# A four-sequence transformer block with a top-k mask on one NeuronCore: where five small pieces of work stand

## The chip, the cores and the metric

One NeuronCore of a Trainium2 chip runs the whole program. The metric is the device time of one execution in microseconds (us). Engines are named as the profile names them: PE is TensorE (PEld its weight loads), DVE is VectorE, ACT is ScalarE, POOL is GpSimd, SP is SyncE, which issues most DMAs. The five engines run their own instruction lists and meet only at semaphores.

## The reference

Four sequences of 512 rows of 512 numbers. For each sequence, first a mask from a top-k, then a transformer block:

```python
adj = emb_s * emb_t * softmax(x, axis=-1) / sqrt(512)      # 512 x 512 per sequence
adj[diag] = -inf
x = x + (1.0 where adj is among its 5120 largest of the sequence, else 0)
ada = timestep_embed @ ada_w + ada_b                        # shift, scale, gate, twice
x1 = ln(x) * (1 + scale1) + shift1
q, k, v = x1 @ qkv_w + qkv_b                                # 16 heads of 128
attn_out = softmax(q k^T / sqrt(128)) v                     # then @ out_w + out_b
y = x + gate1 * attn_out
x2 = ln(y) * (1 + scale2) + shift2
y = y + gate2 * (gelu(x2 @ ffn_w1 + b1) @ ffn_w2 + b2)      # hidden width 2048
out = x + y
```

All is float32. The kernel gets that precision from TensorE by splitting each operand into a high and a low part and adding three products.

## The kernel before

**The matrix work.** The program is written out for sequences 0, 1, 2, 3, one after the other. Every product is three matmuls (`mm3`: high by high, high by low, low by high; L1387, L1388, L1389), each 128 by 128 weights against 512 columns (256 where only half of the rows is done, `ROWS[0]` or `ROWS[1]`). In a head h PE does: 12 matmuls of scores q k^T, then q and k of head h+1 (24), one tile of v for head h+4 (12), and the product of probabilities and v of head h-1 (12, `attend`, done is counted in `pv_done`): 60 in all. From head 12 on v tiles give way to pieces of the output projection. After head 15 come the rest of that projection (`wide(b, "out", u, ...)`, u = 0 to 3, 16 pieces `kc` each, result columns in four banks of PSUM), its way back (`transpose_back`), the second layer norm (z), `mlp_in` and `mlp_out`.

**The weights.** Halves of 1 MB are loaded by SP into four places, (region 0 or 1, half 0 or 1), from a DRAM scratch in which they lie split. Only sequence 0 finds them unsplit: there ScalarE writes the high part (`split_hi`), then GpSimd the low part (`split_lo`, L661), and saves follow. A unit of the output projection is two such halves: half 0 holds kc 0 to 7, half 1 kc 8 to 15.

**The softmax of a head** runs on three engines: VectorE finds row maxima (L1217), ScalarE the exponentials (L884), VectorE reciprocals, ScalarE and VectorE the high and low halves of 16 bits (L891, L1232), SP transposes them with a DMA, and GpSimd widens them to `probT` (`widen`, L741). VectorE then makes the low parts of q and k of the next head (`qk_part`, L1188), without which PE can't start its scores, and the low parts of v and of the head's result.

**The top-k** of sequence b+1 runs beneath sequence b. In heads 0 to 4 VectorE finds the softmax's maxima, multiplies (`topk_adj`, L1062), and turns values into keys that sort as integers (`topk_keys`, two passes per tile, L1071 and L1073); GpSimd puts minus infinity on the diagonal between the two (`clear_diagonal`, L652). Then 32 steps of a bisection over the threshold `cand`, 16 over the keys' upper 16 bits and 16 over the lower (variable `low`): VectorE counts one half of the keys above `cand` (`cnt_v`, L1028), ScalarE the other (sum of signs, `cnt_s`, L779), PE sums both over partitions (`take_total`, L1399 and L1400), and VectorE moves `cand` (`topk_move`, L1091 and L1094). I call the sum of step s "total s". Totals 0 to 10 stand in heads 5 to 15, totals 11 to 15 amid the output projection, the others in the MLP. After total 15 VectorE makes `low` from the chosen upper level (L1105, L1108). The top-k of sequence 0 runs alone at the start and has a form of its own (`is_t0`).

What sets the order is the code of each engine, written out by hand; there is no scheduler. `wait_apart` is a wait on a semaphore in an instruction of its own.

## Time and profile before

| | us |
|---|---|
| time, median of 3 runs | 1572.07 (1571.55 to 1572.12) |
| the profiled execution's own time | 1573.86 |
| its span, first to last instruction | 1572.0 |
| PE busy in the span | 1508.5 (96%) |
| DVE busy | 1110.1 (71%) |
| ACT busy | 886.3 (56%) |
| POOL busy | 409.9 (26%) |
| PE in the chain that ended last | 87% of the span |

The busy time of PE counts overlapping matmuls once, and the end of a matmul is modelled: in a dense stretch matmuls start every 0.23 us while each is shown 0.39 us long. So lost time of PE is read from the distances of starts and from the waits, not from the busy share. Sequence 0's block begins at about 100 us, sequence 1's at 482 us, sequence 2's at 848 us, and sequence 3's at 1210 us.

### The profile page before, as it was taken

How to read it: one execution, taken by the hardware profiler on the slowest of the kernel's cores; microseconds unless marked ns; L12 is line 12 of the kernel's file. 1: busy time of each engine (PE TensorE's matmuls, PEld its weight loads, DVE VectorE, ACT ScalarE, POOL GpSimd, SP SyncE). 2: the span in 40 equal slices, each digit the busy share in tenths (PEclk: the TensorE clock that was granted, in tenths of full speed). 3: DMA queues.
4: the chain of work that ended last, by engine and by line, in shares of the span. 5: the costliest groups of instructions: out<-in, count | busy, mean ns of one | idle time of the engine just before them, and what ended most of it. 6: DMA issues, size and time to landing. Idle time of an engine off the chain costs nothing.

```text
span 1572.0 us, 21300 instructions
## 1 busy us (share of the span) xinstructions
PE 1508.5 (96%) x7253; PEld 1250.4 (80%) x7253; DVE 1110.1 (71%) x2328; ACT 886.3 (56%) x1631; POOL 409.9 (26%) x243
## 2 busy tenths in 40 slices
PE   1999889999999999999999999999999999999998
PEld 1877778778778888887878888887978888888987
DVE  7878978876786887775775887775777666664431
ACT  4557577774754666663672766664572556554240
POOL 6713635454120322221000232221000122222000
PEclk9999999999999999999999999999999999999999
DMA  7867869998666788685455777677454787776463
GB/s 289 314 242 195 237 171 261 247 219 299 216 231 238 170 214 215 165 206 176 175 219 205 199 207 208 163 214 208 168 201 170 220 201 160 209 210 156 176 237 123
DMA packets 334507, 327.58 MB, mean 208 GB/s; under 512 B 270752, under 2 KB 275008, under 8 KB 331328
## 3 DMA queue, kind: packets, MB, share of 16 engines
q1 hardware_dynamic: 334112, 325.90, 69.3%
q8 instruction: 58, 0.95, 0.2%
q14 instruction: 49, 0.40, 0.1%
q10 hardware_dynamic: 288, 0.33, 0.1%
HBM read 204.54 MB, written 54.54 MB: 165 GB/s over the span
## 4 chain that ended last, share of the span: by engine, by line
PE 87%; DVE 7%; DMA 2%; DVEq 1%; ACT 1%; issue 1%; SPq 1%; POOL 0%; ACTq 0%; POOLq 0%
PE bank L1387 26%; PE bank L1388 26%; PE bank L1389 26%; PE bank L1701 2%; DMA w<-split_weights 1%; DVE halves L1232 1%; DVE tb L1028 1%; PE bank L1604 1%; PE bank L1599 1%; PE bank L1600 1%; PE bank L1416 1%; DVEq L1218 1%; SPq L537 1%; DVE adj L1073 1%; DVE tb L1071 1%
## 5 line engine op out<-in xcount | busy, mean ns | idle before, releaser
L741 POOL CAST probT<-turned 128x2048 fp32r<-128x2048 f16 x128 | 244.3, 1924 | 700.8 <-DMA turned<-halves 395.3
L1387 PE MATMUL bank<-xT,w 128*128 128x512 f32 x704 | 281.0, 399 | 2.0 <-POOL w L661 2.0
L1388 PE MATMUL bank<-xT,w 128*128 128x512 f32 x704 | 275.6, 391 | 0.0
L1389 PE MATMUL bank<-xT,w 128*128 128x512 f32 x704 | 275.3, 391 | 0.0
L884 ACT ACTIVATE prob<-bank,nbias 128x512 f32<-128x512 f32 x256 | 176.4, 690 | 119.8 <-DVE nbias L1219 110.5
L1232 DVE SCALAR_TENSOR_TENSOR halves<-prob,rinv,halves 128x512 f16<-128x512 f32 x256 | 176.7, 752 | 25.2 <-ACT halves L891 24.9
L1217 DVE TENSOR_REDUCE rowmax<-bank 128x1 f32<-128x512 f32 x256 | 174.4, 681 | 0.0
L891 ACT ACTIVATE halves<-prob,rinv 128x512 f16<-128x512 f32 x256 | 164.1, 711 | 17.1 <-DVE rinv L1228 15.3
L1389 PEld LDWEIGHTS bank<-xT,w 128*128 128x128 f32 x704 | 133.0, 189 | 28.2
L1387 PEld LDWEIGHTS bank<-xT,w 128*128 128x128 f32 x704 | 132.9, 189 | 28.0 <-POOL w L661 2.4
L1388 PEld LDWEIGHTS bank<-xT,w 128*128 128x128 f32 x704 | 133.0, 189 | 25.5
L661 POOL TENSOR_TENSOR w<-wraw,w 128x1024 fp32r<-128x1024 f32 x38 | 95.5, 2518 | 179.2 <-ACT w L820 178.9
L1387 PE MATMUL bank<-act,w 128*128 128x512 f32 (+1 forms) x320 | 114.1, 357 | 3.8 <-DMA w<-split_weights 3.8
L1188 DVE SCALAR_TENSOR_TENSOR act<-bank,small,act 128x512 fp32r<-128x512 f32 x64 | 47.9, 748 | 94.6 <-ACT act L911 94.6
L779 ACT ACTIVATE passed_s<-adj,cand 128x1024 bf16<-128x1024 uint16 (+1 forms) x64 | 73.8, 1153 | 70.9 <-DVE cand L1094 41.1
L1388 PE MATMUL bank<-act,w 128*128 128x512 f32 (+1 forms) x320 | 111.5, 348 | 0.0
L1389 PE MATMUL bank<-act,w 128*128 128x512 f32 (+1 forms) x320 | 111.5, 348 | 0.0
L911 ACT ACTIVATE act<-bank,small 128x512 fp32r<-128x512 f32 x64 | 44.0, 688 | 116.0 <-PE bank L1389 115.9
L779 ACT ACTIVATE passed_s<-low,cand 128x1024 bf16<-128x1024 f32 (+1 forms) x64 | 74.0, 1156 | 55.4 <-DVE cand L1094 24.6
L1387 PE MATMUL bank<-qk 128*128 128x512 f32 x256 | 99.9, 390 | 5.5 <-DVE qk L1188 5.2
L1387 PE MATMUL bank<-w,act 128*128 128x512 f32 x256 | 101.5, 396 | 0.0
L1188 DVE SCALAR_TENSOR_TENSOR qk<-bank,small,qk 128x512 fp32r<-128x512 f32 x128 | 90.3, 744 | 14.9 <-ACT qk L876 8.6
(173 smaller groups left out, 3342.4 us busy)
## 6 DMA issues: line engine op xcount, KB each, us to landing
w<-split_weights SPq DMA_DIRECT2D x154, 1024.0 KB, 6.0
split_weights<-w SPq DMA_DIRECT2D x38, 1024.0 KB, 6.7
wraw<-weights_in SPq DMA_DIRECT2D x48, 512.0 KB, 4.8
split_weights<-xT SPq DMA_DIRECT2D x7, 1024.0 KB, 7.8
adaw<-ada_w_in SPq DMA_DIRECT2D x4, 1536.0 KB, 12.6
xr<-x_in SPq DMA_DIRECT2D x4, 1024.0 KB, 6.3
split_weights<-qk SPq DMA_DIRECT2D x3, 1024.0 KB, 7.8
adj<-x_in SPq DMA_DIRECT2D x3, 1024.0 KB, 7.9
```

Source lines behind the costliest of these rows:

```text
L661: nc.gpsimd.tensor_tensor(w[:, region, 1, span], wraw[:, k % 2, :], w[:, region, 0, span].bitcast(F32), ALU.subtract)\
L741: nc.gpsimd.tensor_copy(probT[:, :, :, rows].rearrange("p a j (i t) -> p i (a j) t", i=2), turned_of(h)[:, 2 * pair:2 * pair + 2, :, :]).t ...
L779: nc.scalar.activation(passed_s[:, :2 * NCOUNT - at], src, ACT.Sign, bias=cand[:, :], scale=-1.0, accum_out=cnt_s[:, :]).then_inc(counted_ ...
L884: nc.scalar.activation(prob[:, i, :], bank[i][:, :], ACT.Exp, bias=nbias[:, i:i + 1], scale=SCALE, accum_out=rowsum[:, i:i + 1]).then_inc( ...
L891: nc.scalar.mul(halves_of(h)[:, i, 0, :], prob[:, i, :], rinv[:, i:i + 1]).then_inc(p16_hi, 1)
L911: nc.scalar.activation(act[:, 0, h, :], bank[6][:, :], ACT.Identity, bias=col("bv", h))\
L1188: return V.scalar_tensor_tensor(dst, src, bias, hi.bitcast(F32), ALU.add, ALU.subtract)
L1217: V.reduce_max(rowmax[:, i:i + 1], bank[i][:, :], AX.X)
L1232: V.scalar_tensor_tensor(halves_of(h)[:, i, 1, :], prob[:, i, :], rinv[:, i:i + 1], halves_of(h)[:, i, 0, :], ALU.mult, ALU.subtract).then ...
L1387: pe.matmul(dst, w_hi_ap, x_hi_ap, start=first, stop=False)
L1388: pe.matmul(dst, w_hi_ap, x_lo_ap, start=False, stop=False)
L1389: return pe.matmul(dst, w_lo_ap, x_hi_ap, start=False, stop=last)
```

## The change

Five edits, in the order of the program:

1. **Keys ahead of q, k.** In heads 1 to 4 VectorE's top-k passes (`topk_under_head`) stand ahead of `qk_part` of the next head, instead of behind it.
2. **Clearing of the diagonal** of tiles 0 and 1 moves on GpSimd from head 0 to behind the widening of head 1, of tiles 2 and 3 from head 1 to head 2. In sequence 0 the split of unit 5's first half also waits for all eight tiles of z.
3. **One matmul for both counts.** `cnt_v` and `cnt_s` become two columns of one tile `counts`, and PE sums both with one matmul with ones (not for sequence 0's own top-k). The combination of the two sums is made by one more VectorE instruction of one column ahead of the comparison.
4. **Level change in one pass.** GpSimd scales the lower 16 bits into `low` when all heads are done (`next_low`), for each sequence as already for sequence 0's own top-k; VectorE then needs one pass over 2048 columns in place of two. The lower level's numbers are scaled by 2^-17 throughout.
5. **Unit 3's first rows amid unit 2.** PE does pieces 0 to 7 of unit 3's first rows between pieces 7 and 8 of unit 2, and the other eight where all sixteen stood.

```diff
@@ GpSimd
+            def next_low(b):
+
+                pool.wait_ge(pv_done, (b + 1) * H)
+                scale_low()
+
...
@@ GpSimd, first_sequence
                     for k in range(at + max(1, n - 1), at + n):
                         split_lo(k)
                     at += n
-                    if h < 2:
-                        clear_diagonal(1, 2 * h, 2 * h + 1)
+                    if h in (1, 2):
+                        clear_diagonal(1, 2 * h - 2, 2 * h - 1)
+                next_low(0)
                 for k in range(at, NHALF):
                     if ORDER[k] == unit_half(5, 0):
                         first_rows_lo(0)
+                        wait_apart(pool, z_ready, 2 * NT)
                     split_lo(k)
@@ GpSimd, later sequences
                     widen(b, h)
-                    if b < B - 1 and h < 2:
-                        clear_diagonal(b + 1, 2 * h, 2 * h + 1)
+                    if b < B - 1 and h in (1, 2):
+                        clear_diagonal(b + 1, 2 * h - 2, 2 * h - 1)
+                if b < B - 1:
+                    next_low(b)
                 first_rows_lo(b)
@@ VectorE, topk_move
-                    V.tensor_scalar(step_up[:, :], total(step)[:, 0:1], float(KTOP - P * NCOUNT // 2) - 0.5, bit,
-                                    ALU.is_gt, ALU.mult)
+                    bit *= unit(step)
+                    V.tensor_scalar(step_up[:, :], total(step)[:, 1:2], 0.5, float(KTOP - P * NCOUNT // 2) - 0.5,
+                                    ALU.mult, ALU.add)
+                    dve.drain()
+                    V.tensor_scalar(step_up[:, :], total(step)[:, 0:1], step_up[:, :], bit, ALU.is_gt, ALU.mult)
...
-                    if is_t0(t):
-                        dve.wait_ge(low_scaled, 1)
-                        V.scalar_tensor_tensor(low[:, :], keys16[:, :, 1], cand[:, :], low[:, :],
-                                               ALU.subtract, ALU.add)
-                    else:
-                        V.tensor_scalar(low[:, :], keys16[:, :, 1], cand[:, :], float(1 << 17),
-                                        ALU.subtract, ALU.mult)
-                        dve.drain()
-                        V.tensor_tensor(low[:, :], low[:, :], keys16[:, :, 0], ALU.add)
+                    dve.wait_ge(low_scaled, t + 1)
+                    V.scalar_tensor_tensor(low[:, :], keys16[:, :, 1], cand[:, :], low[:, :], ALU.subtract, ALU.add)
@@ VectorE, head
+                dve.drain()
+                if not last and 0 < h < FIRST_TOTAL:
+                    topk_under_head(b + 1, h)
                 if h + 1 < H:
                     qk_part(b, h + 1)
                 dve.drain()
-                if not last:
+                if not last and not 0 < h < FIRST_TOTAL:
                     topk_under_head(b + 1, h)
@@ PE, take_total
-                pe.matmul(total(step)[:, 0:1], weight_v[:, :], cnt_v[:, :], start=not is_t0(t), stop=False)
-                pe.matmul(total(step)[:, 0:1], weight_s[:, :], cnt_s[:, :], start=False, stop=True)\
-                    .then_inc(total_ready, 1)
+                if is_t0(t):
...
+                else:
+                    pe.matmul(total(step)[:, 0:2], ones[:, :], counts[:, :], start=True, stop=True)\
+                        .then_inc(total_ready, 1)
@@ PE, output projection
-                    wide(b, "out", 2, parts[r], parts[r + 1], y_done)
+                    if r == 1:
+                        wide(b, "out", 2, 6, 8, y_done)
+                        wide(b, "out", 3, 0, 8, y_done, ROWS[0])
+                        wide(b, "out", 2, 8, 10, y_done)
+                    else:
+                        wide(b, "out", 2, parts[r], parts[r + 1], y_done)
...
-                wide(b, "out", 3, 0, KC, y_done, ROWS[0])
+                wide(b, "out", 3, 8, KC, y_done, ROWS[0])
```

VectorE at the end of head 3 of sequence 0, before (L1232 the low halves, L1188 the low parts of q and k or of a head's result, L1071 and L1073 the two passes over the keys of a tile):

```order
L1232 SCALAR_TENSOR_TENSOR halves_0_69<-prob,rinv,halves_0_69 128x512 x4
L1188 SCALAR_TENSOR_TENSOR qk<-bank,small,qk 128x512 x2
L1071 TENSOR_SCALAR tb<-adj 128x512
L1073 TENSOR_TENSOR adj<-adj,tb 128x512
L1071 TENSOR_SCALAR tb<-adj 128x512
L1073 TENSOR_TENSOR adj<-adj,tb 128x512
L1183 SCALAR_TENSOR_TENSOR v<-bank,v 128x512
```

The same place after the change (lines are some five to nine further down):

```order
L1237 SCALAR_TENSOR_TENSOR halves_0_69<-prob,rinv,halves_0_69 128x512 x4
L1080 TENSOR_SCALAR tb<-adj 128x512
L1082 TENSOR_TENSOR adj<-adj,tb 128x512
L1080 TENSOR_SCALAR tb<-adj 128x512
L1082 TENSOR_TENSOR adj<-adj,tb 128x512
L1193 SCALAR_TENSOR_TENSOR qk<-bank,small,qk 128x512 x2
L1188 SCALAR_TENSOR_TENSOR v<-bank,v 128x512
```

The four passes over keys now stand between the halves and q, k.

GpSimd at the end of the heads of sequence 0, before (L661 the low part of a half unit of weights, L741 the widening of a head, L678 the low part of the first rows):

```order
L661 TENSOR_TENSOR w<-wraw,w 128x1024 x2
L741 CAST probT<-turned_1_72 128x2x8x128 x2
L661 TENSOR_TENSOR w<-wraw,w 128x1024 x5
L678 TENSOR_TENSOR xT<-tmp,xT 128x256 x4
```

And after:

```order
L661 TENSOR_TENSOR w<-wraw,w 128x1024 x2
L748 CAST probT<-turned_1_72 128x2x8x128 x2
L661 TENSOR_TENSOR w<-wraw,w 128x1024
L688 TENSOR_SCALAR low<-adj 128x2048
L661 TENSOR_TENSOR w<-wraw,w 128x1024 x4
L678 TENSOR_TENSOR xT<-tmp,xT 128x256 x4
```

The first split behind the widening is unit 2's second half; the scaling of `low` has come between it and the split of unit 3's first half.

PE in the output projection around total 13, before (L1539 turns a column block back, then the total, then pieces of unit 2):

```order
L1539 MATMUL bank<-ident,yT 128x128 x4
L1399 MATMUL bank<-cnt_v,ones 128x1
L1400 MATMUL bank<-cnt_s,minus_half 128x1
L1387 MATMUL bank<-act,w 128x512
L1388 MATMUL bank<-act,w 128x512
L1389 MATMUL bank<-act,w 128x512
L1387 MATMUL bank<-act,w 128x512
L1388 MATMUL bank<-act,w 128x512
L1389 MATMUL bank<-act,w 128x512
L1387 MATMUL bank<-act,w 128x512
```

And after:

```order
L1550 MATMUL bank<-ident,yT 128x128 x4
L1411 MATMUL bank<-counts,ones 128x2
L1395 MATMUL bank<-act,w 128x512
L1396 MATMUL bank<-act,w 128x512
L1397 MATMUL bank<-act,w 128x512
L1395 MATMUL bank<-act,w 128x512
L1396 MATMUL bank<-act,w 128x512
L1397 MATMUL bank<-act,w 128x512
L1395 MATMUL bank<-act,w 128x256
L1396 MATMUL bank<-act,w 128x256
```

One small matmul is left of two, and behind unit 2's pieces 6 and 7 the half-wide matmuls of unit 3 begin (24 of them stand there).

## Rows read from the trace of the kernel before

**Rows 1.** Busy time by stretch: time, PE, PEld, DVE, ACT, POOL, clock, DMA.
```profile
120.00:500.00 380.00, 363.73 (x1736) 297.13 (x1735) 298.72 (x571) 241.47 (x427) 152.95 (x74) 0.99 0.79 232
500.00:870.00 370.00, 367.46 (x1770) 302.93 (x1770) 271.69 (x577) 214.58 (x402) 67.36 (x40) 1.00 0.66 194
```

**Rows 2.** Waits of PE over the span: total us, times, longest.
```profile
PE bank L1399 <- DVE act L1188: 5.2, 1, 5.2
PE bank L1387 <- DMA w<-split_weights: 3.8, 3, 2.3
PE bank L1416 <- DVE z L1169: 3.1, 2, 1.9
PE bank L1539 <- DVE yT L1250: 1.5, 1, 1.5
```

**Rows 3.** PE's order of time around one total of two counts, and around take_ranks.
```profile
815.01 0.39 PE L1389 MATMUL bank<-w,act 128*128 128x512 f32 x1
...
815.69 0.39 PE L1389 MATMUL bank<-w,act 128*128 128x512 f32 x1
...
816.30 0.40 PE L1388 MATMUL bank<-w,act 128*128 128x512 f32 x1
...
821.30 0.39 PE L1389 MATMUL bank<-w,act 128*128 128x512 f32 x1
...
821.93 0.39 PE L1388 MATMUL bank<-w,act 128*128 128x512 f32 x1
```

**Rows 4.** VectorE in head 3 of sequence 0: start, length.
```profile
172.23 2.51 DVE L1071 TENSOR_SCALAR tb<-adj 128x512 int32<-128x512 int32 x1
...
181.97 0.69 DVE L1183 SCALAR_TENSOR_TENSOR v<-bank,v 128x512 fp32r<-128x512 f32 x1
```

**Rows 5.** PE starts the scores of head 5 of sequence 0.
```profile
192.25 0.47 PE L1387 MATMUL bank<-qk 128*128 128x512 f32 x1 [3.68 <-DVE qk L1188]
```

**Rows 6.** GpSimd in head 3 of sequence 0.
```profile
172.05 4.94 POOL L661 TENSOR_TENSOR w<-wraw,w 128x1024 fp32r<-128x1024 f32 x2 [5.11 <-ACT w L820]
```

**Rows 7.** Granted clock after two waits of PE: stretch, PE, PEclk, DMA.
```profile
200.50:204.00 3.50, 3.50 (x10) 0.50 0.05 19
736.40:739.90 3.50, 3.50 (x13) 0.51 0.02 7
```

**Rows 8.** VectorE in heads 1 and 3 of sequence 1.
```profile
524.01 1.41 DVE L1188 SCALAR_TENSOR_TENSOR qk<-bank,small,qk 128x512 fp32r<-128x512 f32 x2
...
527.49 0.69 DVE L1183 SCALAR_TENSOR_TENSOR v<-bank,v 128x512 fp32r<-128x512 f32 x1
...
550.30 1.40 DVE L1188 SCALAR_TENSOR_TENSOR qk<-bank,small,qk 128x512 fp32r<-128x512 f32 x2
...
554.34 0.69 DVE L1183 SCALAR_TENSOR_TENSOR v<-bank,v 128x512 fp32r<-128x512 f32 x1
```

**Rows 9.** PE starts the scores of head 4 of sequence 1.
```profile
553.55 0.39 PE L1387 MATMUL bank<-qk 128*128 128x512 f32 x1
```

**Rows 10.** GpSimd: the scaling of low, and the end of sequence 0's heads.
```profile
17.95 5.38 POOL L683 TENSOR_SCALAR low<-adj 128x2048 f32<-128x2048 uint16 x1 [4.61 <-DVE cand L1037]
...
364.87 4.75 POOL L661 TENSOR_TENSOR w<-wraw,w 128x1024 fp32r<-128x1024 f32 x2 [8.25 <-ACT w L820]
```

**Rows 11.** PE takes total 13 in sequence 0.
```profile
366.70 0.17 PE L1399 MATMUL bank<-cnt_v,ones 128*128 128x1 f16 x1
```

**Rows 12.** PE's total 15 and VectorE's level change, sequence 1.
```profile
741.33 0.18 PE L1399 MATMUL bank<-cnt_v,ones 128*128 128x1 f16 x1
...
742.10 1.29 DVE L1105 TENSOR_SCALAR low<-adj,cand 128x2048 f32<-128x2048 uint16 x1
743.46 2.29 DVE L1108 TENSOR_TENSOR low<-low,adj 128x2048 f32<-128x2048 f32 x1
...
747.83 0.81 DVE L1250 TENSOR_SCALAR yT<-bank,small,ada 128x512 f32<-128x512 f32 x1
```

**Rows 13.** PE waits for unit 2's second half in sequence 1.
```profile
735.60 0.50 PE L1387 MATMUL bank<-act,w 128*128 128x512 f32 x1 [2.33 <-DMA w<-split_weights]
```

More of the change, by code:

```diff
@@ L204, in count_split, with unit @@
     return FIRST_V if is_t0(t) else NCOUNT
-def unit(t, step):
-    return UNIT if is_t0(t) and step >= LEVEL else 1.0
+def unit(step):
+    return UNIT if step >= LEVEL else 1.0
 def first_splits(h):
@@ L312, in block_kernel @@
         offset = new("offset", [P, 1], F16)
-        cnt_v = new("cnt_v", [P, 1], F16)
-        cnt_s = new("cnt_s", [P, 1], F16)
+        counts = new("counts", [P, 2], F16)
+        cnt_v, cnt_s = counts[:, 0:1], counts[:, 1:2]
         sign_sum = new("sign_sum", [P, 1], F16)
@@ L787, in topk_sides @@
                                          accum_out=sign_sum[:, :]).then_inc(signs_summed, 1)
-                nc.scalar.mul(far_cand[:, :], cand[:, :], -FAR / unit(t, LEVEL)).then_inc(far_ready, 1)
+                nc.scalar.mul(far_cand[:, :], cand[:, :], -FAR / unit(LEVEL)).then_inc(far_ready, 1)
                 act_e.wait_ge(far_ready, t * 2 + 1)
                 act_e.wait_ge(ties_counted, t + 1)
-                nc.scalar.activation(low[:, :], low[:, :], ACT.Identity, bias=far_cand[:, :], scale=FAR / unit(t, LEVEL))\
+                nc.scalar.activation(low[:, :], low[:, :], ACT.Identity, bias=far_cand[:, :], scale=FAR / unit(LEVEL))\
                     .then_inc(far_ready, 1)
@@ L1030, in count @@
                 if is_t0(t):
-                    far = TOP_BIT / (1 << step % LEVEL) / 2 * unit(t, step)
+                    far = TOP_BIT / (1 << step % LEVEL) / 2 * unit(step)
                     V.tensor_scalar(bounds[:, 0:1], cand[:, :], -far, None, ALU.add)
@@ L1036, in start_level @@
             def start_level(t, step):
-                V.memset(cand[:, :], (TOP_BIT - 0.5) * unit(t, step)).then_inc(cand_ready, 1)
+                V.memset(cand[:, :], (TOP_BIT - 0.5) * unit(step)).then_inc(cand_ready, 1)
                 dve.drain()
@@ L1393, in take_total @@
                     pe.wait_ge(cand_ready, step + 1)
-                weight_v, weight_s = (big, minus_half_big) if is_t0(t) else (ones, minus_half)
                 if is_t0(t):
@@ L1398, in take_total @@
                 pe.wait_ge(counted_s, t * STEPS + (step + 1))
-                pe.matmul(total(step)[:, 0:1], weight_v[:, :], cnt_v[:, :], start=not is_t0(t), stop=False)
-                pe.matmul(total(step)[:, 0:1], weight_s[:, :], cnt_s[:, :], start=False, stop=True)\
-                    .then_inc(total_ready, 1)
+                if is_t0(t):
+                    pe.matmul(total(step)[:, 0:1], big[:, :], cnt_v[:, :], start=False, stop=False)
+                    pe.matmul(total(step)[:, 0:1], minus_half_big[:, :], cnt_s[:, :], start=False, stop=True)\
+                        .then_inc(total_ready, 1)
+                else:
+                    pe.matmul(total(step)[:, 0:2], ones[:, :], counts[:, :], start=True, stop=True)\
+                        .then_inc(total_ready, 1)
             def take_ranks(t):
```

## The prediction

> **What bounds the kernel now.** I read first the table of busy time by stretch [rows 1]. From 120 us on PE is the bound: in 500 to 870 it idles 2.5 of 370 us, in 120 to 500 (sequence 0) 16.3 of 380. So only two things count: work that PE itself loses or gains, and PE's waits. The list of waits, read next [rows 2], with one more row for q, k [rows 5], names them: 3.7 us and 5.2 us on VectorE in sequence 0, 1.9 on z, 1.5 on a gated column block, and three waits for weight loads, 3.8 in sum, the longest 2.3 in sequence 1 [rows 13]. Third, the clock: after the wait of 5.2 us and after that of 2.3 us stretches of 3.5 us show a granted clock of 0.50 and 0.51 [rows 7], that is 1.2 GHz of 2.4, though PE is never idle in them. Each costs half of 3.5, about 1.75 us. No such stretch follows the wait of 3.7 us at once, so a wait may or may not cost this.
>
> The pace of a full matmul is 0.227 us: three starts in 0.68 us [rows 3]. A head's 60 are 13.6 us.
>
> **One matmul for both counts.** From 815.69 to 816.30 PE starts one full matmul, the two small ones and another full one: 0.61 us, of which 0.45 are the full ones, so the pair costs 0.16. Around take_ranks, with three small ones, the same distance is 0.63 [rows 3]. One small matmul more or less is thus 0.02 to 0.03 us. There are 32 totals in each of three sequences: 96 x 0.025 = 2.4 us saved. Bounds: nothing, if the 0.16 is the price of any interruption, and 7.5 us, if half of each pair's 0.16 goes. I take 2.4, because the three-matmul row is the same situation one step further.
> The Trainium skill (TensorE: Matmul & The Clock Gate, "LDWEIGHTS (loading the stationary operand)") prices a weight load at columns/1.2 ns, 107 ns for 128 columns; were each removed load exposed, this edit would give 10 us. The rows above speak against it.
>
> **The instruction added to each step.** One more VectorE instruction of one column with its drain lies between a total and the new `cand`. From total 15 at 741.33 to the level change at 742.10 [rows 12] pass 0.77 us, in which two such instructions stand and the way over the semaphore, so I take 0.24 for one more. It is hidden where PE has 2.7 us between totals. It shows where only nine matmuls (2.0 us) stand between totals 14 and 15, and where a head's q, k were already late. I take +0.3 us beyond what is in the terms below; bounds 0 and 3.
>
> **Keys ahead of q, k, sequence 0.** In head 3 the four key passes begin at 172.23 and the next work at 181.97: 9.7 us [rows 4]. In sequence 1 the same four fill 551.7 to 554.34, 2.6 us [rows 8]. The difference is GpSimd, which splits weights from 172.05 for 4.94 us [rows 6] and then widens: the first pass took 2.51 us, which is the length of one of GpSimd's two splits. So VectorE's head 4 ran late, its q, k held PE until 192.25 [rows 5], and the count and the low part of head 3's result, behind another slow tile, until 5.2 us later [rows 2]. Put ahead of q, k the passes start 1.4 us earlier: the first tile (1.3 us) is through before GpSimd starts, the second waits out both splits to 177.0 and ends at 177.4, and q, k end at 178.8. Add 1.2 us for head 2, where the multiplications meet the split in the same way: 180.0. PE could start head 4 at 192.25 - 3.68 - 13.6 = 175.0, so a new wait of 5 us stands here. Head 5 then starts at 193.6, and the total that came after the wait of 5.2 us comes at 196.3 instead of 200.2. The slow stretch of 1.75 us stays, behind another wait. Gain 3.9, rounded to 4 us. A wait of PE on a split in head 1, which stood behind the diagonal's clearing, also goes, but head 1's q, k are as much later (two multiplications and their small instructions, 2.1 us in [rows 8]); I let these cancel. Bounds: 9 us gained if the passes meet no split, 1 lost if both tiles do.
> The Trainium skill (SBUF — State Buffer, "Who interferes with whom") says that VectorE with two SBUF inputs and GpSimd exclude each other for the whole of an instruction, and the earlier starter wins. By that rule the split delays the second tile exactly as above; the trace agrees with it (2.51 us against 2.6 for four passes).
>
> **The same in sequences 1 and 2.** No wait of VectorE's making exists there to be cured. Head 1's q, k end at 525.42 and the next work starts at 527.49, so the moved passes are 2.1 us; head 3's end at 551.7, moved passes 2.6 [rows 8]. PE starts head 4 at 553.55 [rows 9] and head 2 at 553.55 - 27.2 = 526.35. So q, k would be ready at 527.5 and 554.3: 1.1 and 0.8 us late. VectorE's work per head is unchanged (it only swaps order), so from head 2 on the lateness is mostly shared, not added: a PE that is 1.2 us late gives all of it back as slack at the next head. I get 1.3 us per sequence, 2.6 in sum. Bounds: 0, if the engine has this slack, and 8, if each of four heads adds its 1.0 us.
>
> **Level change and unit 3's rows, sequence 0.** This is the largest term and it is a loss. GpSimd is strictly in order: the split of unit 2's second half (from 364.87, half of 4.75 us, to 367.25), then now the scaling, 5.38 us as at 17.95 [rows 10], to 372.6, then the split of unit 3's first half, 2.4, to 375.0. PE takes total 13 at 366.70 [rows 11], does six matmuls, and wants unit 3 at 368.2: it waits 6.8 us, and a slow stretch adds 1.75. Behind it the split of unit 3's second half, whose high part ScalarE makes only after its count, meets VectorE's level change; PE then waits some 3.5 us for the gated block in place of 1.5 [rows 2]. The wait of 1.9 on z goes, since GpSimd now stays off. 6.8 + 1.75 + 3.5 - 1.5 - 1.9 = 8.6, of which I take 8 for what overlaps. Bounds: 2 (the wait short and unslowed) and 12.
>
> **The same in sequences 1 to 3.** Here GpSimd is free and the scaling is hidden behind unit 0 to 2's matmuls (it takes 5.4 us from the end of the last head, and total 15 comes later than unit 2's thirteenth piece). Unit 3's first half was issued ahead of the load that ends PE's wait at 735.60 [rows 13], so it is there, and 24 half-wide matmuls (2.7 us) cover the waits of 3.8 us and their slow stretch of 1.75: -5.55. But half of unit 3's cover is gone from behind total 15. VectorE's gated block ends at 748.64, 7.3 us after total 15 [rows 12]; PE had 9 matmuls and 48 half-wide ones there, about 7.7 us, and now has 24, about 4.9. The one pass costs 2.3, as a pass with two inputs does, against 1.29 + 2.29 and a gap [rows 12], so VectorE needs 7.3 - 1.35 + 0.24 = 6.2: a new wait of about 1.2 us in sequences 1 and 2, and 0.2 each at total 15. -5.55 + 2.4 + 0.4 = -2.8 us. Bounds: -5.5 and +1.
>
> **Sum.** -2.4 + 0.3 - 4 + 2.6 + 8 - 2.8 = +1.7 us. The profiled execution took 1573.86 us (span 1572.0 and 1.9 around it) and would take 1575.6; it lies 1.8 above the median of the runs, so on their scale 1572.07 + 1.7 = 1573.8 us. A difference of 0.2%, 3.1 us, is about what can be told from none.
>
> **Rivals.** (A) PE's wait for unit 3 in sequence 0 doesn't hold, because the scaling starts as soon as head 15 is done and is over by the time it is wanted. GpSimd idled 8.25 us before 364.87 [rows 10], which speaks for it; that the split of unit 2's second half stands ahead of the scaling in its list speaks against. Without the term: 1565.8 us. (B) Small matmuls cost more than the comparison of two and three shows, and half of each pair's 0.16 us goes: 5.1 us more, 1568.7. For it: the slow start of the full matmul behind a pair. Against: the same slow start behind three. (C) Slower: the lateness of q, k adds up. Place: heads 1 to 4 of sequences 1 and 2. Price: 1.0 us x 8 heads = 8 instead of 2.6, so 1579.2. It decides as soon as VectorE's moved passes (2.1 and 2.6 us) exceed the slack between q, k and the scores (0.9 us at head 2, 1.85 at head 4, [rows 8, 9]) at each head anew, which happens if its work behind q, k waits for a PE result that now comes later too. For it: the low part of a head's result does wait for PE. Against: that wait is short.
>
> **How the numbers follow.** Forecast 0.51, A 0.19, B 0.08, C 0.22. The forecast's own size is uncertain by some 4 us (the unit 3 term by 3, the head terms by 2 each), so I count 0.41 of it within 3.1 us and 0.10 slower. A and B are faster: 0.27. Slower: 0.22 + 0.10 = 0.32. Range 1565 to 1580: from A to just beyond C.
>
> **What will show it.** In the new profile: PE's full matmuls one small matmul apart 96 times; in sequence 0 one wait of about 5 us on q, k at head 4 and none before the first total of the next top-k; a wait of about 7 us on GpSimd's split near 366 to 375; no wait on weight loads; VectorE's waits of about 1 us on q, k in heads 2 to 5 of sequences 1 and 2 and on the gated block. I am wrong if the 7 us wait is missing, or if the heads of sequence 1 lose nothing.

## The result: 1581.0 us, slower by 0.55%, outside the range

| | before | after |
|---|---|---|
| median | 1572.09 us (4 runs, 1571.55 to 1572.53) | 1581.04 us (4 runs, 1577.58 to 1583.27) |
| ratio | | 1.0055, 95% interval 1.0035 to 1.0075 |
| profiled execution, its span | 1573.86, 1572.0 | 1583.27, 1581.4 |
| mean granted clock in the span | 0.996 | 0.991 (its other runs 0.993 to 0.995) |

In the terms of the sum the changed kernel is 8.6 us slower (0.0055 x 1572), where +1.7 was forecast. Measured once more in other rounds it stood at 1.0045 (1.0027 to 1.0063), +7.1 us. One execution of the kernel with edit 4 alone, 2780 us at a mean granted clock of 0.81, is left out of its median and its ratio.

The profile of the changed kernel first lists PE's waits (total us, times, longest), the answer to [rows 2]; those of the first top-k are left out:

```profile
PE bank L1395 <- DVE qk L1193: 12.5, 7, 3.7
PE bank L1395 <- POOL w L661: 7.5, 2, 6.6
PE bank L1550 <- DVE yT L1258: 4.6, 3, 1.9
...
PE bank L1427 <- DVE z L1174: 2.0, 1, 2.0
...
PE bank L1395 <- issue: 0.7, 2, 0.3
```

The wait of 5.2 us at the first total and the 3.8 us for weight loads are gone, as forecast. There are now seven waits on q, k in place of three (12.5 us for 5.2), one of 6.6 us on GpSimd's split, and three on the gated block in place of one. By stretch (time, PE, PEld, DVE, ACT, POOL, clock, DMA), the answer to [rows 1]:

```profile
120.00:500.00 380.00, 360.61 (x1668) 295.10 (x1667) 294.69 (x598) 238.55 (x424) 156.03 (x75) 0.97 0.77 223
500.00:870.00 370.00, 366.89 (x1745) 302.06 (x1744) 275.77 (x606) 213.51 (x400) 70.93 (x41) 1.00 0.67 200
```

In sequence 0 PE is busy 3.1 us less than before in the same 380 us, and while busy it has the lower clock: 0.97 against 0.99. Sequence 1's stretch is nearly as before. Sequence by sequence, by PE's first matmul of each MLP (L1599, now L1610): before they start at 389.71, 757.15, 1119.07 and 1478.51, now at 402.12, 765.88, 1130.23 and 1488.03. So sequence 0 loses 12.4 us, sequence 1 gives 3.7 back, sequence 2 loses another 2.4, and sequence 3 gives back 1.6; a second profile of the changed kernel, which loses 10.5 us in sequence 0, shows the other three within 0.2 us. Of the 12.4 us the waits account for 5.0 (19.3 for 14.3 us from 101 us on): more than half of the loss in sequence 0 is not in the list of waits at all. Here are four stretches of the changed kernel, each at or behind the end of one of its waits (same columns):

```profile
148.60:155.40 6.80, 6.62 (x17) 5.21 (x18) 4.94 (x13) 2.50 (x7) 3.29 (x4) 0.53 0.59 219
182.70:189.50 6.80, 5.86 (x15) 4.63 (x16) 5.09 (x11) 3.29 (x7) 5.27 (x3) 0.53 1.07 388
373.90:380.70 6.80, 5.97 (x27) 5.89 (x28) 0.00 (x0) 0.00 (x0) 0.77 (x1) 0.53 0.71 230
394.30:397.70 3.40, 3.40 (x20) 3.40 (x19) 2.66 (x10) 0.37 (x2) 2.61 (x2) 0.56 0.62 133
```

A full matmul starts every 0.43 us in them, every 0.23 elsewhere. With one more of 3.4 us at 101 they make 27.2 us at half clock (the second profile of the same kernel shows 20.4); before there were 13.7. The forecast had looked at two windows of 3.5 us [rows 7]; it missed a stretch behind the 2.0 us wait of head 1, and that the one in its first window begins while PE still waits:

```profile
149.40:152.80 3.40, 3.40 (x10) 2.63 (x9) 2.93 (x7) 2.92 (x7) 2.57 (x2) 0.50 0.88 308
197.20:204.00 6.80, 3.55 (x10) 2.87 (x11) 5.86 (x14) 4.89 (x11) 1.59 (x1) 0.50 0.50 201
```

These are single executions, and the profiled one of the changed kernel has the lowest clock of its four. Over all executions on record the mean granted clock is 0.9937 for the changed kernel (9 executions) and 0.9950 for the one before (92): 0.0013 of 1572 us, some 2 us.

The waits themselves, in their order. PE at head 2 of sequence 0, and what VectorE and GpSimd did there:

```profile
148.78 0.77 PE L1395 MATMUL bank<-qk 128*128 128x512 f32 x1 [3.74 <-DVE qk L1193]
```
```profile
143.60 3.57 DVE L1071 SCALAR_TENSOR_TENSOR adj<-tb,factor,adj 128x512 f32<-128x512 f32 x2
147.27 1.41 DVE L1193 SCALAR_TENSOR_TENSOR qk<-bank,small,qk 128x512 fp32r<-128x512 f32 x2
```
```profile
144.27 2.36 POOL L661 TENSOR_TENSOR w<-wraw,w 128x1024 fp32r<-128x1024 f32 x1 [7.17 <-ACT w L829]
```

Two multiplications now stand ahead of q, k and take 3.57 us, because a split starts within the first of them, 0.03 us before its end, and holds up the second; q, k end at 148.7 and PE starts at 148.78. At head 4 the wait is 3.43. The output projection of sequence 0, GpSimd and then PE, the answers to [rows 10] and [rows 11]:

```profile
364.62 2.39 POOL L661 TENSOR_TENSOR w<-wraw,w 128x1024 fp32r<-128x1024 f32 x1 [8.32 <-ACT w L829]
366.97 5.38 POOL L688 TENSOR_SCALAR low<-adj 128x2048 f32<-128x2048 uint16 x1
372.32 2.35 POOL L661 TENSOR_TENSOR w<-wraw,w 128x1024 fp32r<-128x1024 f32 x1
```
```profile
366.45 0.17 PE L1411 MATMUL bank<-counts,ones 128*128 128x2 f16 x1
...
374.73 0.58 PE L1395 MATMUL bank<-act,w 128*128 128x256 f32 x1 [6.64 <-POOL w L661]
```

This is the forecast's 6.8 us wait to 0.2 us. Behind total 15 in sequence 0 and in sequence 1, the answer to [rows 12]:

```profile
385.65 4.09 DVE L1113 SCALAR_TENSOR_TENSOR low<-adj,cand,low 128x2048 f32<-128x2048 uint16 x1
...
752.67 2.35 DVE L1113 SCALAR_TENSOR_TENSOR low<-adj,cand,low 128x2048 f32<-128x2048 uint16 x1
```
```profile
392.69 0.66 PE L1550 MATMUL bank<-ident,yT 128*128 128x128 f32 x4 [1.90 <-DVE yT L1258]
...
757.97 0.66 PE L1550 MATMUL bank<-ident,yT 128*128 128x128 f32 x4 [1.34 <-DVE yT L1258]
```

The one pass takes 2.35 us where GpSimd is free, and 4.09 where a split (385.22 to 387.60) meets it. PE waits 1.34 us in sequences 1 and 2 (forecast 1.2). The last row answers to [rows 3], a total in the MLP:

```profile
818.17 0.39 PE L1397 MATMUL bank<-w,act 128*128 128x512 f32 x1
818.40 0.18 PE L1411 MATMUL bank<-counts,ones 128*128 128x2 f16 x1
...
818.75 0.39 PE L1396 MATMUL bank<-w,act 128*128 128x512 f32 x1
```

From full to second full matmul pass 0.58 us with one small one, 0.61 with two, 0.63 with three.

### The profile page after: what moved, and what is told of

Read it like the earlier page. It is cut to its first block, busy times and chain, and to the rows that moved or that the text cites. A ratio compares the mean times of both kernels' runs of the same rounds, so it can differ in the third digit from the quotient of the medians.

```text
span 1581.4 us, 21362 instructions
## 1 busy us (share of the span) xinstructions
PE 1511.4 (96%) x7157; PEld 1253.0 (79%) x7157; DVE 1120.2 (71%) x2421; ACT 885.3 (56%) x1631; POOL 420.1 (27%) x246
## 4 chain that ended last, share of the span: by engine, by line
PE 84%; DVE 9%; DVEq 3%; ACT 1%; issue 1%; POOL 1%; DMA 1%; SPq 0%; ACTq 0%
PE bank L1395 25%; PE bank L1397 25%; PE bank L1396 25%; PE bank L1717 2%; DVE tb L1037 1%; DVE halves L1237 1%; DVEq L1223 1%; PE bank L1615 1%; PE bank L1610 1%; PE bank L1611 1%; PE bank L1427 1%; DVE low L1113 1%; DVE adj L1082 1%; PE bank L1449 1%; PE bank L1446 1%
## 5 line engine op out<-in xcount | busy, mean ns | idle before, releaser
L661 POOL TENSOR_TENSOR w<-wraw,w 128x1024 fp32r<-128x1024 f32 x38 | 94.4, 2485 | 201.4 <-ACT w L829 199.9
L1395 PE MATMUL bank<-act,w 128*128 128x512 f32 (+1 forms) x320 | 115.6, 361 | 7.5 <-POOL w L661 7.5
L1395 PE MATMUL bank<-qk 128*128 128x512 f32 x256 | 102.6, 401 | 13.2 <-DVE qk L1193 12.5
L1396 PE MATMUL bank<-act,w 128*128 128x512 f32 (+1 forms) x320 | 112.6, 352 | 0.0
L1397 PE MATMUL bank<-act,w 128*128 128x512 f32 (+1 forms) x320 | 112.6, 352 | 0.0
L1193 DVE SCALAR_TENSOR_TENSOR qk<-bank,small,qk 128x512 fp32r<-128x512 f32 x128 | 90.6, 747 | 19.3 <-ACT qk L885 7.9
L1397 PE MATMUL bank<-qk 128*128 128x512 f32 x256 | 101.6, 397 | 0.0
```

The costliest lines, as they stand in the source:

```text
L661: nc.gpsimd.tensor_tensor(w[:, region, 1, span], wraw[:, k % 2, :], w[:, region, 0, span].bitcast(F32), ALU.subtract)\
L1193: return V.scalar_tensor_tensor(dst, src, bias, hi.bitcast(F32), ALU.add, ALU.subtract)
L1395: pe.matmul(dst, w_hi_ap, x_hi_ap, start=first, stop=False)
L1396: pe.matmul(dst, w_hi_ap, x_lo_ap, start=False, stop=False)
L1397: return pe.matmul(dst, w_lo_ap, x_hi_ap, start=False, stop=last)
```

## The experiments

Two theories stood after the result. **Theory 1, the clock:** the new waits of PE bring more time at half clock than the one stretch that was priced. **Theory 2, the sizes:** some edit costs or gives other than forecast, by its waits and passes alone. "Us" below is the ratio to before, taken in the same rounds, times 1572; in brackets its 95% interval.

### Each edit alone

Edit 3 alone, one matmul for both counts (the edit as in the diff above, without the lower level's scale):

```diff
+                    pe.matmul(total(step)[:, 0:2], ones[:, :], counts[:, :], start=True, stop=True)\
+                        .then_inc(total_ready, 1)
```

> The kernel before with edit 3 alone (one matmul for both counts, and VectorE's added instruction). Theory 1 (the changed kernel is 9 us slower because PE's new waits cost more half clock than I gave them: its trace shows 27.3 us at half clock against 13.7 before): this edit makes no new wait, so its time is the 96 small matmuls alone, 2.4 to 3 us less, 1569.1 to 1569.7 us, with the clock and the scatter of before (0.996, under 1 us). Theory 2 (the parts of my sum themselves were too small, each of them): the added instruction shows at totals 14 and 15 and in late heads, and the edit gives 0 to 1 us, 1571 to 1572 us.

Measured: 1568.65 us (12 runs), ratio 0.9976 (0.9966 to 0.9987): -3.8 us, somewhat more than theory 1 gave it and far from theory 2.

Edits 1 and 2 alone (keys ahead, clearing one head later; not the wait for z):

> The kernel before with edits 1 and 2 alone (keys ahead of q, k, diagonal cleared one head later; the wait on z is left as before). The trace of the changed kernel shows waits on q, k of 3.7, 0.8 and 3.4 us in sequence 0 and of 1.1 to 1.7 and 0.3 us in sequences 1 and 2. Theory 1: by their lengths the heads come out at -2 in sequence 0 and +3.7 in the others, +2 us; with two half-clock stretches of 6.8 us behind the first two waits in place of those of before another +2, so 1575 to 1577 us, with a scatter of 2 us or more and the granted clock at 0.994 to 0.996. Theory 2: +2 us at an unchanged clock and small scatter, about 1574.

Measured: 1574.48 us (12 runs), 1.0012 (1.0000 to 1.0023): +1.9 us, on the wrong side of the forecast of -1.4. It came with no lower clock (0.9957 in the mean, 0.9949 for before in the same rounds), as theory 2 said: here the clock is not the cause.

Edit 4 alone, the level change in one pass:

> The kernel before with edit 4 alone (level change in one pass, GpSimd scales low). In sequence 0 unit 3's first half is split 5.4 us later, at about 375.0, while PE wants it at 374.4, behind unit 2: a wait of 0.6 us. The level change is 1.3 us shorter, which takes most of the 1.5 us wait on the gated block. Both theories: 1571 to 1572 us, no new half clock. It tells whether the scaling alone hurts: if it does, by 4 us or more, the order of GpSimd's list is the fault without edit 5.

Measured: 1575.52 us (11 runs), 1.0016 (1.0001 to 1.0032): +2.5 us, where both theories expected no loss.

Edit 5 alone, unit 3's first rows amid unit 2, with the level change in two passes:

> The kernel before with edit 5 alone (unit 3's first rows amid unit 2). In sequence 0 its split ends at 369.7 and PE wants it at 368.2, so 1.5 us of wait instead of 6.6; the loads' waits of 3.8 us go. The level change keeps its two passes (3.65 us), so PE waits some 2.4 us for the gated block in sequences 1 and 2 and more in sequence 0. Theory 1: waits +1.5 +3 +2 x 2.4 -3.8, +5.5 us, with half clock gone behind the load (-1.7) but perhaps come back behind the others: 1575 to 1579 us. Theory 2: +5.5 us, 1577, with a small scatter.

Measured: 1582.24 us (6 runs), 1.0056 (1.0040 to 1.0073): +8.8 us, as much as the whole change and more than either theory's +5.5 us of waits; its mean clock is 0.9923. Its waits:

```profile
PE bank L1539 <- DVE yT L1250: 7.8, 3, 3.2
PE bank L1387 <- POOL w L661: 4.3, 4, 2.0
```

The gated block's wait, 1.5 us once before, is now 7.8 in three: the half-wide matmuls taken from behind total 15 had covered VectorE's level change. So edit 5 needs edit 4 in sequences 1 and 2. In the whole kernel it costs about as much with edit 4 (7 to 9 us, from the run without edit 5 below) as without.

Edit 2 alone, the clearing one head later with the keys behind q, k:

```diff
-                    if h < 2:
-                        clear_diagonal(1, 2 * h, 2 * h + 1)
+                    if h in (1, 2):
+                        clear_diagonal(1, 2 * h - 2, 2 * h - 1)
```

> The kernel before with edit 2 alone: the clearing of the diagonal one head later, keys behind q, k. The changed kernel with keys behind q, k again stood at 1.0095 of before and the changed kernel at 1.0045 to 1.0055, and there PE waited 3.1, 3.5, 2.0 and 2.1 us in heads 2 to 5 ahead of the 5.2. Theory 1 and this reading: edit 2 alone costs 6 to 8 us (1.004 to 1.005), and edit 1 mostly repays it; that is, the two together stand at +1.3 to +1.9 because they are two terms of opposite sign. Theory 2, on which the prediction rested: edit 2 alone costs nothing (it removes a wait of 2 us), 0.999 to 1.0.

Measured: 1582.23 us (6 runs), 1.0046 (1.0029 to 1.0064): +7.2 us. Why, the multiplications of head 1 and GpSimd beside them show. Before (VectorE, then GpSimd):

```profile
143.52 1.41 DVE L1062 SCALAR_TENSOR_TENSOR adj<-tb,factor,adj 128x512 f32<-128x512 f32 x2
```
```profile
144.45 1.53 POOL L652 TENSOR_SCALAR_AFFINE_SELECT adj<-adj 128x512 f32<-128x512 f32 x2 [8.67 <-DVE adj L1062]
145.95 2.35 POOL L661 TENSOR_TENSOR w<-wraw,w 128x1024 fp32r<-128x1024 f32 x1
```

With edit 2 alone:

```profile
146.99 4.60 DVE L1062 SCALAR_TENSOR_TENSOR adj<-tb,factor,adj 128x512 f32<-128x512 f32 x2
```
```profile
144.50 2.40 POOL L661 TENSOR_TENSOR w<-wraw,w 128x1024 fp32r<-128x1024 f32 x1 [7.17 <-ACT w L820]
146.85 1.90 POOL L741 CAST probT<-turned 128x2048 fp32r<-128x2048 f16 x1
```

Before, GpSimd stood 8.67 us at the clearing, waiting for the multiplication, and so could start neither the split nor the widening beside it: the wait kept the two engines apart. It took little: ScalarE's part of the split came at 144.5, as GpSimd's first row with edit 2 alone shows, and the clearing held the split back to 145.95. Without it both run into VectorE's multiplications, 4.60 us in place of 1.41, in head 1 and again in head 2 (4.59); PE then waits 3.1, 3.5 and 3.4 us on q, k and 3.9 at the first total, 13.9 us in sum for 10.9 before. That is 3 of the 7.2 us; some 2.4 more go with the clock, whose mean is 0.9927 in these runs and 0.9942 for before in the same rounds. The counterpart is the changed kernel with edit 1 undone, that is with the keys behind q, k again, and edit 2 kept:

> The changed kernel with the four key passes of heads 1 to 4 behind q, k again (the diagonal's clearing stays one head later). Prediction's terms: 4 us of gain in sequence 0 and 2.6 of loss in sequences 1 and 2, so the kernel would be 1.4 us slower, 1582.5. Theory 2 (the keys' move costs where a gain was forecast; alone it stood at 1574.5 against 1573.2): 1 to 2 us faster, 1579 to 1580. Theory 1 (clock) says in addition that in sequence 0 it comes to the number of waits, not to their length: two waits of 3.7 and 3.4 us become waits of 3.7 and 5.2, with as much half clock, so within 1.5 us of the changed kernel.

Measured: 1586.42 us (6 runs), 1.0095 (1.0075 to 1.0116): 0.0040 to 0.0050 above the changed kernel's two ratios, 6 to 8 us slower than it. The prediction's terms and both theories missed here. Edit 2 costs about 7 us and edit 1 gives 5 to 8 of them back. Edit 1 without edit 2 was not run.

### Where unit 3's rows cost

Rows where they stood before in every sequence, edits 1 to 4 kept:

> The changed kernel with all of unit 3's first rows where they stood before, in every sequence; the other four edits stay. If the edits add up, the sum of the single runs gives 1573.15 - 4.5 (one matmul) + 1.3 (keys and diagonal) + 2.5 (level change) = 1572.4 us. Theory 1 (clock): no new half-clock stretch in the output projections, 1570 to 1573. Theory 2: the 10 us found above the forecast sit elsewhere as well, 1574 to 1577. Against the same kernel with rows moved only in sequences 1 to 3: whichever is faster tells whether the move ever pays.

Measured: 1570.87 us (12 runs), 0.9998 (0.9985 to 1.0010): -0.3 us. Rows moved only in sequences 1 to 3:

```diff
-                    if r == 1:
+                    if r == 1 and not is_first(b):
...
-                wide(b, "out", 3, 8, KC, y_done, ROWS[0])
+                wide(b, "out", 3, 0 if is_first(b) else 8, KC, y_done, ROWS[0])
```

> The changed kernel, but in sequence 0 unit 3's first rows stay where they stood before; in sequences 1 to 3 they stand amid unit 2. The wait of 6.6 us on GpSimd's split goes, and with it 6.8 us at half clock, and the cover behind total 15 is back (that wait was 1.9 and a stretch of 3.4 us). Theory 1 (clock counts): 6.6 + 3.4 = 10 us less, up to 12 with the second place, 1569 to 1572 us. Theory 2 (only the length of the waits counts): 6.6 to 7 less, 1574 to 1575 us. If the excess sits in sequences 1 to 3 the gain is smaller still, 1577 or more.

Measured: 1569.63 us (11 runs), 0.9987 (0.9975 to 0.9998): -2.0 us. Both came where theory 1 expected them. So the move is worth about -1.7 us in sequences 1 to 3 (the two intervals overlap) and costs 9 to 11 us in sequence 0 (1.0045 to 1.0055 against 0.9987), from a wait of 6.6 and 0.9 on the splits and 10.2 us at half clock.

### The clock by itself

Fillers are extra full matmuls whose results are overwritten. They end about when the awaited data come, so the wait stays as long and only the clock can differ.

```diff
+                        if is_first(b):
+                            filler(2, 28)
                         wide(b, "out", 3, 0, 8, y_done, ROWS[0])
```

The changed kernel again, and beside it the same with these 28:

> The changed kernel itself, once more, in the same rounds as the kernel with fillers ahead of unit 3, so that the two can be set against each other. Both theories expect the ratio of the first measurement, 1.0055 of before, with the granted clock of its executions between 0.990 and 0.995 where before has 0.993 to 0.997.

> The changed kernel with the 28 filler matmuls ahead of unit 3's first rows in sequence 0 alone; the waits ahead of head 2 and head 4 stay empty. Theory 1 (clock): the 6.8 us at half clock that follow this one wait go, 3.4 us less than the changed kernel measured beside it, ratio to before about 1.003; the stretch of 3.4 us behind the gated block may go with it (1.7 more). Theory 2 (length of the wait alone): the same time as the changed kernel within 1 us, ratio 1.005 to 1.006.

Measured: 1579.51 (5 runs, 1578.31 to 1581.22) and 1576.77 (8 runs, 1574.85 to 1578.49), ratios 1.0045 and 1.0030: 2.7 us less, as theory 1 had it. At 373.5 to 380.3 and 393.0 to 396.4 the filled kernel shows 1.00. All three long waits of sequence 0 filled:

> The changed kernel, with extra full matmuls whose results are overwritten, so that PE is busy in its three long waits of sequence 0: 16 ahead of head 2's scores (the wait is 3.7 us), 15 ahead of head 4's (3.4 us), 28 of them ahead of unit 3's first rows (6.6 us). They give the data no earlier, so the waits' own length stays lost. Theory 1 (clock): behind these three waits the changed kernel shows 6.8 us each at a granted clock of 0.5, 20.4 us in sum; with PE busy they stay at 1.0 and up to 10 us come back. Between 1571 and 1575 us, and less scatter. Theory 2 (the waits' length alone, and too small terms elsewhere): the time stays, 1580 to 1583 us, since the fillers take exactly what the waits took.

Measured: 1574.95 us (12 runs), 1.0026 (1.0014 to 1.0038): 3 to 4.6 us below the changed kernel's two ratios, not the 10 that theory 1 allowed. 3.4 us at 101 and at 165 stay at half clock in it, and no filler matches its wait exactly.

The cleanest pair is a candidate without edits 1, 2 and 4 (next section), as it is and with 33 fillers ahead of head 5's scores and the first total:

> The candidate itself, beside its filled form. Both theories: 0.9963 of before, as measured.

> The candidate (one matmul for both counts; the last sequence's first rows of unit 3 amid unit 2) with 16 filler matmuls ahead of head 5's scores and 17 ahead of the first total, in sequence 0: PE's waits of 3.7 and 4.0 us are filled, their length stays. Theory 1 (clock): the 6.8 us at half clock that lie from the scores of head 5 to behind the total go, 3.4 us less than the candidate measured beside it, 0.994 of before. Theory 2 (length alone): the same as the candidate, 0.996.

Measured: 1566.44 (5 runs, 1565.78 to 1567.76) and 1562.69 (6 runs, 1560.76 to 1564.17); the two sets of runs do not overlap. The ratios to before in the same rounds are 0.9947 (0.9930 to 0.9965) and 0.9920; the candidate's own had been forecast at 0.9963. The stretches at 193.2 and 200.0, unfilled:

```profile
193.20:196.60 3.40, 3.40 (x10) 2.63 (x9) 3.32 (x2) 0.00 (x0) 3.40 (x2) 0.51 1.28 206
200.00:206.80 6.80, 5.83 (x15) 4.57 (x16) 5.53 (x18) 4.52 (x12) 0.00 (x0) 0.50 0.18 73
```

and filled:

```profile
193.20:196.60 3.40, 3.40 (x16) 2.81 (x15) 3.32 (x2) 0.00 (x0) 3.40 (x2) 1.00 1.00 187
200.00:206.80 6.80, 5.70 (x26) 4.74 (x27) 5.53 (x18) 4.52 (x11) 0.00 (x0) 1.00 0.28 115
```

PE's first total in each, unfilled and filled:

```profile
200.97 0.19 PE L1405 MATMUL bank<-counts,ones 128*128 128x2 f16 x1 [3.60 <-DVE act L1190]
```
```profile
201.10 0.18 PE L1406 MATMUL bank<-counts,ones 128*128 128x2 f16 x1 [1.36 <-DVE act L1191]
```

The first stretch costs nothing: four of the 16 matmuls in its filled row are fillers, and the total waits for VectorE until 201 us in both. In the second 11 more matmuls fit, times 0.227 us, 2.5 us. The profiles stand 3.5 us apart at the first MLP, the medians 3.75; the rest is shorter waits on q, k in later heads. So theory 1 holds for these waits, with its price: a stretch at half clock costs half of the part in which PE works, and what PE does in it ahead of a further wait on another engine is free.

### A version that beats both, and the keys in sequence 0

Edit 3, and edit 5 in the last sequence alone, where no top-k runs beneath:

```diff
-                    if r == 1:
+                    if r == 1 and last:
```

> A candidate: the kernel before with edit 3 (one matmul for both counts) and, in the last sequence alone, unit 3's first rows amid unit 2. The last sequence has no top-k beneath it, so no level change waits for the cover that is moved, and its wait for a weight load (0.85 us in the run with edit 3 alone) goes. Both theories: edit 3's measured ratio of 0.9976, and 0.8 us less, 0.997 of before, 1567 us. Theory 1 allows up to 1.7 more where that wait brought a half-clock stretch, which it did not.

Measured: 1566.44 us (10 runs), 0.9963 (0.9952 to 0.9974): -5.8 us against before, the fastest kernel without fillers. The same with edits 1 and 2 in sequence 0 only:

> The same candidate, and in sequence 0 alone the keys ahead of q, k with the diagonal's clearing one head later. In sequence 0 the waits of PE in the heads fell with it from 10.9 to 8.0 us; in sequences 1 and 2, where it brought new waits of 1.1 and 1.2 us, the order stays as before. Theory 2 (lengths of waits): 2 to 3 us below the candidate without it, 0.995 of before. Theory 1 (clock): the single run showed 13.6 us at half clock with and 13.7 without, but three waits and no more than three count; edit 3 alone had brought that down to 10 us. So 0 to 3 us below the candidate without it, not more.

Measured: 1567.37 us (11 runs), 0.9972 (0.9962 to 0.9983), 1.4 us above the candidate without them, with overlapping intervals. And that one with its waits filled:

> The candidate with the keys ahead of q, k in sequence 0, with fillers ahead of the scores of heads 2 (16) and 4 (15), where PE waits 3.7 and 3.4 us. What is asked is where the gain of the shorter waits went (0.9972 with the keys ahead, 0.9963 without). Theory 1 (clock): it went into stretches at half clock behind two waits that did not stand there before; filled, it should be at 0.994 to 0.995, as low as or below the candidate with its own waits filled. Theory 2: it is lost in the waits of head 2 and head 3 themselves and in sequences 1 and 2; filled it stays at 0.997.

Measured: 1564.06 us (6 runs), 0.9931 (0.9913 to 0.9950), against 0.9920 for the filled candidate. Filling did not bring the keys' gain forward; but this kernel's mean clock is 0.9980 with fillers and the candidate's 0.9992, so up to 1.9 us of clock are left in the comparison. Without fillers both have 0.996, and there the clock is not what ate the gain. With the keys ahead the profile is 1.2 us ahead of the candidate when sequence 0 ends (the wait on z at 392.43 against 393.63) and 1.3 behind at 1094. Between them lies one pass of head 3 of sequence 2, in code that is the same in both. Keys ahead in sequence 0 (VectorE, GpSimd, PE):

```profile
914.34 2.40 DVE L1073 TENSOR_TENSOR adj<-adj,tb 128x512 int32<-128x512 int32 x1
```
```profile
914.31 1.90 POOL L741 CAST probT<-turned 128x2048 fp32r<-128x2048 f16 x1 [8.67 <-DMA turned<-halves]
```
```profile
931.85 0.18 PE L1408 MATMUL bank<-counts,ones 128*128 128x2 f16 x1 [1.57 <-DVE act L1190]
```

The candidate:

```profile
914.81 0.69 DVE L1073 TENSOR_TENSOR adj<-adj,tb 128x512 int32<-128x512 int32 x1
```
```profile
914.96 4.25 POOL L741 CAST probT<-turned 128x2048 fp32r<-128x2048 f16 x2 [8.68 <-DMA turned<-halves]
```

GpSimd's widening starts 0.03 us ahead of the pass in the one and 0.15 us behind it in the other, and the pass takes 2.40 or 0.69 us. The filled pair shows the same, 2.41 us with the keys ahead (the widening 0.02 us ahead of the pass) and 0.69 without, and the wait of 1.5 us at the total stands in both kernels with the keys ahead and in none of the three profiles without. So the gain of sequence 0, 1.2 us in the profiles, was lost by chance of timing in sequence 2. That this is the whole difference of the medians (0.9 us, within their intervals) is argued from profiles, not shown.

## Why the prediction was wrong, step by step

| term | forecast | measured |
|---|---|---|
| one matmul for both counts, with its added instruction | -2.1 | -3.8 (-5.3 to -2.0) |
| keys ahead, sequence 0 | -4 | +1.4 by the pair of candidates (0.9972 - 0.9963, intervals overlap): about -1.2 in sequence 0 and +2.5 in sequence 2, by their profiles |
| keys ahead, sequences 1 and 2 | +2.6 | about +0.5 (1.9 for edits 1 and 2 everywhere, less 1.4) |
| unit 3 and level change, sequence 0 | +8 | 9 to 11, and part of the next row |
| the same, sequences 1 to 3 | -2.8 | -1.7 for the rows; edit 4 +1.6 over the sum of edits 1 to 3 (-0.3 + 3.8 - 1.9) |
| sum | +1.7 | +7.1 and +8.6 |

**The step that failed** first is "I let these cancel" in the keys' term. The prediction priced the moved multiplications of head 1 at the 2.1 us they take in sequence 1, and took the clearing's removal for a gain, since it removed a wait of PE of 2.0 us. It was the other way round: the clearing had kept GpSimd off the multiplications. They now take 3.57 us and PE waits 3.74 for them, at a head where no wait was forecast. With the clearing moved and nothing else the kernel is 7.2 us slower. The wait at head 4 came (3.4, forecast 5) and the wait at the first total went, but the heads' waits fell only from 10.9 to 8.0 us, 1 us less than forecast, and in the pair of candidates from 9.7 to 8.5. The other part of this term's miss, the late pass in sequence 2, no step of the prediction could have priced: it hangs on hundredths of a us. The rule of exclusion that the prediction applied to head 3 had to be applied to head 1 too. (The pass of 2.51 us reads one SBUF tile, `adj`, so it is no instance of what the prediction cites for it, which speaks of two inputs; the rows show that such passes are held up as well.)

**The second miss is the clock.** "A slow stretch adds 1.75" was counted once in sequence 0 and taken off once in sequence 1, so that the sum held no change of clock. Behind the wait for unit 3 stood 6.8 us of it and behind the gated block 3.4; and "the slow stretch stays, behind another wait" in the heads became two of 6.8 in one profile and two of 3.4 in the other. The waits of the unit 3 term came to 6.6 + 0.9 + 1.9 - 1.5 - 1.9 = 6.0 us, less than the 6.9 forecast; with the 7.0 to 8.9 us that PE worked at half clock there in the two profiles, 3.5 to 4.5 us of cost and not 1.75, they make the measured 9 to 11. For the whole kernel the profiles say 3 to 7 us (13.7 against 20.4 to 27.2 at half clock), the mean clock of all executions some 2, and filling the waits returned 3 to 4.6. The largest single gap to the forecast is the keys' term, not this one.

That the first median lies outside the range is narrow, 1581.04 against 1580, and the second ratio would put it at 1579.2, within; the forecast of no clear change was wrong in both.

**Right** were: the wait for the split in sequence 0 in mechanism and length (6.64 for 6.8), against rival A, which did not happen; the level change slowed by the split in sequence 0, though PE's wait behind it was 1.9 us and not 3.5; no wait for weight loads; 1.34 for 1.2 us behind total 15 in sequences 1 and 2. The small matmul's price of 0.03 us was read rightly from rows with two and three, and the row with one now agrees: -2.9 of the measured -3.8; the rest is within its interval, and neither rival B (-7.5) nor a fully exposed weight load (10 us) fits. In sequences 1 and 2 the wait of 1.1 at head 2 came as worked out in the one (1.11) and longer in the other (1.73), and none of the later ones grew (0.35 and 0.33 at head 3, none listed at heads 4 and 5), so rival C is wrong, though its time, 1579.2, is the closest of the four.

What stays open: edit 4's +1.6 us alongside edits 1 to 3. Their profile shows a wait of 1.26 us on the split of unit 3 at 373, behind the scaling, which is most of it; the profile of edit 4 alone shows the same wait (1.25). Edit 4 was not tried with the scaling issued elsewhere, nor edit 1 with the clearing left where it stood.

## What to carry to other kernels

Before you move a piece of work from an in-order engine, ask what its wait has been holding back: here a clearing of 0.8 us, placed behind VectorE's multiplication, kept 4 us of GpSimd's work from colliding with it, and moving it cost 7 us until another edit repaid most of it. Price a new wait of the busiest engine at its length plus what the clock takes behind it, for each wait anew, and check that price by filling one wait with idle work. Take the clock's share from the mean granted clock of many executions: here a single profile showed 13.5 us more at half clock, and the mean of all executions some 4. A reorder that helps in the later repetitions can lose everything in the first, where data are not yet prepared: guard it by repetition and time each part by itself.

## What the runs showed of the hardware

- Stretches at 1.2 GHz came as 3.4 or 6.8 us, at the end of waits of PE of 1.5 to 6.6 us or just behind them, and not at each: the changed kernel's wait of 3.74 us at head 2 had 6.8 in one profile and 3.4 in another, and the candidate's wait of 2.02 us at 149 had 3.4 in one and none in another.
- Part of the scatter goes with the clock. Over the 92 executions of the kernel before, the time falls by 1.2 us for each 0.001 of mean granted clock, which accounts for 44% of its variance; over the changed kernel's 9 it is 1.3 us and 84%.
- Filling waits with matmuls that compute nothing made the kernel faster: 1562.69 us, 0.9920 of before (0.9902 to 0.9938), against 1566.44 and 0.9947 without them in the same rounds.
- A key pass of 0.69 us took 2.40 when GpSimd had started 0.03 us ahead of it, and 0.69 when GpSimd started 0.15 us behind. Two multiplications of 1.41 us together took 4.60 beside GpSimd's widening. A key pass with one SBUF input (L1071), 0.43 us where GpSimd is idle, took 2.51 beside a split.
